# A vision block on one core: first mean, second mean and half of the output projection moved directly behind a block of scores or minima, into another PSUM bank

## The reference

```python
h = h + attention(layernorm(h))     # 16 heads of 16, stablemax3, then w_out, b_out
h = h + ffn(layernorm(h))           # 4 experts of 1024 hidden, relu, weighted by a gate per token
```

## Time and profile before

| | before |
|---|---|
| median of 3 runs | 3930.28 us (3929.3 to 3931.45) |
| profiled execution | 3926.76 us, span 3925.0 us |
| PE busy | 3863.5 us, 98% |
| PE weight loads | 3394.5 us, 86% |
| GpSimd busy | 2819.8 us, 72% |
| VectorE busy | 2817.5 us, 72% |
| ScalarE busy | 2379.7 us, 61% |
| chain that ended last | 95% PE |

### The profile page before, as it was taken

How to read it: one execution, slowest core, us unless ns; L and a number is a source line. 1 busy time by engine, 2 the same in 40 slices (tenths; PEclk the granted TensorE clock), 3 DMA queues, 4 the chain that set the end, 5 groups by cost and what they waited for, 6 DMA issues and landing times.

```text
span 3925.0 us, 86888 instructions
## 1 busy us (share of the span) xinstructions
PE 3863.5 (98%) x30148; PEld 3394.5 (86%) x30148; DVE 2817.5 (72%) x4316; ACT 2379.7 (61%) x4388; POOL 2819.8 (72%) x3543
## 2 busy tenths in 40 slices
PE   7899999999999999999999999999999999999998
PEld 4788888888888888888888888888888888888887
DVE  6777777777777777777777777777777777777763
ACT  5665566655566655666555666556665556665562
POOL 5666777767777667777677776677776777766676
PEclk9999999999999999999999999999999999999999
DMA  7344444444444444444444444444544444444454
GB/s 243 95 136 142 135 134 142 136 140 140 125 140 139 137 139 137 133 144 135 142 138 127 140 139 137 138 134 135 143 135 143 137 129 141 136 140 125 137 149 140
DMA packets 776546, 545.55 MB, mean 139 GB/s; under 512 B 157624, under 2 KB 701752, under 8 KB 775096
## 3 DMA queue, kind: packets, MB, share of 16 engines
q1 hardware_dynamic: 771416, 539.70, 47.0%
q10 hardware_dynamic: 4704, 0.30, 0.1%
HBM read 518.48 MB, written 21.30 MB: 138 GB/s over the span
## 4 chain that ended last, share of the span: by engine, by line
PE 95%; POOL 1%; DVE 1%; ACT 1%; issue 1%; DMA 0%; ACTq 0%; SPq 0%; POOLq 0%; DVEq 0%
PE ps L1343 67%; PE ps L1427 5%; PE ps L1442 5%; PE ps L1456 5%; PE ps L1541 4%; PE ps L1550 3%; PE ps L1558 2%; PE ps L1519 1%; PE ps L1525 1%; PE ps L1531 1%; PE ps L1507 1%; PE ps L1513 1%; ACT probs L716 0%; DVE lows L1052 0%; PE ps L1339 0%
## 5 line engine op out<-in xcount | busy, mean ns | idle before, releaser
L1343 PE MATMUL ps<-xn,w1s 128*128 128x197 f32 x4096 | 909.7, 343 | 4.6 <-ACT hT L681 2.3
L1343 PEld LDWEIGHTS ps<-xn,w1s 128*128 128x128 f32 x4096 | 676.3, 189 | 144.0 <-issue 132.4
L1343 PE MATMUL ps<-hT,w_s 128*128 128x197 f32 x4064 | 783.8, 330 | 7.6 <-issue 7.3
L977 DVE SCALAR_TENSOR_TENSOR probs<-probs,ps 99x788 f32<-99x788 f32 x512 | 483.3, 970 | 322.5 <-ACT probs L716 322.5
L1343 PEld LDWEIGHTS ps<-hT,w_s 128*128 128x128 f32 x4064 | 691.7, 190 | 9.6 <-issue 7.9
L572 POOL TENSOR_TENSOR hT<-hT 128x197 f32<-128x197 f32 x508 | 331.8, 653 | 505.7 <-ACT hT L696 502.5
L1343 PE MATMUL ps<-xt,w1s 128*128 128x197 f32 x3072 | 681.2, 330 | 3.3 <-ACT hT L687 1.7
L565 POOL TENSOR_SCALAR hT<-hT 128x394 f32<-128x394 f32 x512 | 641.2, 1252 | 17.7 <-DVE hT L1099 17.7
L1052 DVE TENSOR_REDUCE lows<-ps 99x8 f32<-99x1576 f32 (+1 forms) x256 | 460.3, 1799 | 218.6 <-PE ps L1442 218.5
L1343 PE MATMUL ps<-hT,w_a 128*128 128x197 f32 x3048 | 591.0, 329 | 0.2 <-DVE yw L1117 0.2
L1343 PEld LDWEIGHTS ps<-xt,w1s 128*128 128x128 f32 x3072 | 538.2, 190 | 35.9 <-DVE hT L1105 3.4
(11 more groups left out here) (142 smaller groups left out, 6196.7 us busy)
## 6 DMA issues: line engine op xcount, KB each, us to landing
w_s<-w_sums SPq DMA_DIRECT2D x508, 256.0 KB, 3.6
w_a<-in_w SPq DMA_DIRECT2D x384, 256.0 KB, 3.3
w1s<-w_sums SPq DMA_DIRECT2D x512, 192.0 KB, 2.6
w1s<-in_w SPq DMA_DIRECT2D x512, 128.0 KB, 2.3
x<-in_xT SPq DMA_DIRECT2D x30, 1188.0 KB, 7.4
w1s<-in_w SPq DMA_DIRECT2D x512, 64.0 KB, 1.9
w1s<-w_sums SPq DMA_DIRECT2D x512, 64.0 KB, 2.0
out_rows<-rows SPq DMA_DIRECT2D x252, 48.0 KB
```

Of the source, the lines that this page charges most:

```text
L977: nc.vector.scalar_tensor_tensor(out=part, in0=part, scalar=3.75, in1=ps[0:HB, 2 * half:2 * half + 2, 0:N], op0=ALU.add, op1=ALU.mult).the ...
L1343: return mm(place, weights, rows, start=start, stop=True, skip_group_check=True)
```

## The change

Only PE's program and the table of banks change; the queues of the other engines stay as they are.
- The first mean stands directly behind the scores of block 1, one slot of experts ahead of its old place, and writes Y1 for pairs from 2 on. It waits for `h_ready` (the embedding's results have left Y1) instead of `read(3)`. The scores of block 2 no longer wait for `hc_ready`.
- The first half of the output projection stands directly behind the minima of block 3, one slot ahead, in Y1 for pairs from 1 on, and waits for `whole_ready` (the weighed values have left Y1). The second half stays where it was, in bank 1.
- The second mean stands directly behind the minima of block 4, one slot ahead, in Y1 for pairs from 1 on, and waits for `h2_ready`.
- `embed_product(pair + 2, 0)` stays where it is and waits for `hc2_ready` (the second mean has left Y1) instead of `whole_ready`. The minima of block 5 no longer wait for `hc2_ready`.

```diff
--- before.py
+++ after.py
@@ -116,9 +116,9 @@
         HOMES = (dict(embed0=U0, embed1=U1, mean=Y0, var=Y1, q00=U0, k00=Y0, q10=U1, k10=Y1, q01=U0, k01=Y0, q11=U1, k11=Y1, v0=U0, v1=U1,
                       low_t0=0, low_t1=U0, out0=U1, out1=U0, mean2=U1, var2=U1, z=Y0),
                  dict(embed0=2, embed1=3, mean=0, var=1, q00=U1, k00=Y0, q10=U1, k10=Y0, q01=U1, k01=Y0, q11=U0, k11=Y0, v0=Y0, v1=Y1,
-                      low_t0=U0, low_t1=U1, out0=0, out1=1, mean2=0, var2=0, z=0),
-                 dict(embed=Y1, mean=0, var=1, q00=0, k00=1, q10=0, k10=1, q01=0, k01=1, q11=0, k11=1, v0=0, v1=0,
-                      low_t0=1, low_t1=1, out0=0, out1=1, mean2=0, var2=0, z=0))
+                      low_t0=U0, low_t1=U1, out0=Y1, out1=1, mean2=Y1, var2=0, z=0),
+                 dict(embed=Y1, mean=Y1, var=1, q00=0, k00=1, q10=0, k10=1, q01=0, k01=1, q11=0, k11=1, v0=0, v1=0,
+                      low_t0=1, low_t1=1, out0=Y1, out1=1, mean2=Y1, var2=0, z=0))
 
         LOW_HOMES = ((U0, 0, U0, 0, U0, U0, U0, U0), (0,) * 8, (0,) * 8)
 
@@ -1679,13 +1679,13 @@
 
                 if has_b:
                     gap(b, 1, read(2))
-                experts(1)
-                if has_f:
-                    mean(f, read(3))
+                if has_f:
+                    mean(f, (h_ready, at(f, 2, 2)))
+                experts(1)
                 experts(1)
 
                 if has_b:
-                    gap(b, 2, read(4), *([(hc_ready, at(f, 1, 1))] if has_f else []))
+                    gap(b, 2, read(4))
                 experts(1)
                 if has_f:
                     variance(f, read(5))
@@ -1753,25 +1753,26 @@
 
                 if has_f:
                     lowest(f, 3, (low_ready, at(f, 8, 3)), (k_ready, at(f, 4, 4)))
-                experts(1)
                 if has_b:
-                    project_out(b, 0, (low_ready, at(f, 8, 4)) if has_f else read(16))
+                    project_out(b, 0, (whole_ready, at(b, 8, 8)))
+                experts(1)
+                if has_b:
                     project_out(b, 1, (low_ready, at(f, 8, 4)) if has_f else read(16))
                 experts(1)
 
                 if has_f:
                     lowest(f, 4, (low_ready, at(f, 8, 4)), (h2_ready, at(b, 2, 2)))
-                experts(1)
                 if has_b:
-                    mean2(b, (low_ready, at(f, 8, 5)) if has_f else (h2_ready, at(b, 2, 2)))
+                    mean2(b, (h2_ready, at(b, 2, 2)))
+                experts(1)
                 if has_f:
                     lows_to_columns(f, 0, (low_ready, at(f, 8, 5)))
                 if pair + 2 < PAIRS:
-                    embed_product(pair + 2, 0, (whole_ready, at(b, 8, 8)))
-                experts(1)
-
-                if has_f:
-                    lowest(f, 5, (low_ready, at(f, 8, 5)), (q_max_ready, at(f, 4, 2)), (hc2_ready, at(b, 1, 1)))
+                    embed_product(pair + 2, 0, (hc2_ready, at(b, 1, 1)))
+                experts(1)
+
+                if has_f:
+                    lowest(f, 5, (low_ready, at(f, 8, 5)), (q_max_ready, at(f, 4, 2)))
                 experts(1)
                 if has_b:
                     variance2(b, (low_ready, at(f, 8, 6)) if has_f else (hc2_ready, at(b, 1, 1)))
```

More of the change, by code:

```diff
@@ L1763, in step @@
                     lowest(f, 4, (low_ready, at(f, 8, 4)), (h2_ready, at(b, 2, 2)))
+                if has_b:
+                    mean2(b, (h2_ready, at(b, 2, 2)))
                 experts(1)
-                if has_b:
-                    mean2(b, (low_ready, at(f, 8, 5)) if has_f else (h2_ready, at(b, 2, 2)))
                 if has_f:
```

## The result

| | before | after |
|---|---|---|
| median | 3929.3 us (5 runs, 3926.92 to 3931.45) | 4012.13 us (5 runs, 4010.94 to 4014.32) |
| profiled execution, span | 3925.0 us | 4012.5 us |
| mean granted clock of TensorE | 0.996 | 0.990 |
| one pair (start of mean2 to the next) | 120.01 us | 122.24 us, in 12 pairs 123.9 |

The ratio is 1.0212, with a 95% interval of 1.0201 to 1.0223. The time lies inside the range on record, 16 us above the forecast of 3996. Two things make up the 83 us, and both can be read in the trace.

What follows compares the result with a forecast made beforehand. PE, without gaps in the middle, was taken to bound the kernel; the embedding's new wait, 29 x 2.28 = 66 us, on 3926.76 gives 3993, or 3996 against the median, which is 3.5 higher; range 3970 to 4030.

Steps and rivals of the forecast that it cites:

- The decisive step: Embedding's wait for centring L1009: mean2 delays VectorE's down sum, product 2.28 us later per pair, 29 times, 66 us.
- What the moves save: Output projection 0.04 and mean2 0.05 us no longer lost: 0.09 per pair, under 3 us in 31 pairs.
- The early places: Inputs ready at the moved pieces' new places, costing nothing; room 1.8 us at first mean, 0.96 at mean2.
- rival (b): PE's clock falls too, 3.4 us per fall: 4095 if every time, 4030 in a third of the pairs; chance 0.10.
- a granted clock under 1.00 in the middle: Sign of being wrong: PE's granted clock below full in the middle of the trace after; no size given.
- its last sign: If PE's busy time, not its idle time, grew, the reading of the switch cost would be wrong.
- the switch cost: Leaving a tiled block on PE costs 0.11 us, paid by the first whole matmul behind it; no saving taken.
- The rows that I leaned on: Rows 7: PE stall of 2.17 us followed by full clock, 2.93 by half clock; forecast's 2.3 judged nearer the first.
- (a): Embedding's wait there, but VectorE's queue not late by mean2: 1.66 us x 29 = 48 us, 3968 to 3978; chance 0.06.
- (c): Embedding doesn't wait at Y1, as the centring ends ahead of it: about 3922 us; chance 0.02.
- (d): Nothing changes: moved products wait as before, embedding's wait masked by another: 3930 us; chance 0.02.

Runs made afterwards that it cites:

- e2: Kernel before, nothing moved, only the new wait added: the first embedding product of pair + 2 also waits for the second mean's centring; 3975.9 us, ratio 1.0121.
- e7: Changed kernel with the second mean's centring on VectorE put behind the down sum and ahead of the weighting; 3977.7 us, ratio 1.0123.
- e3: Changed kernel with the second mean's centring on VectorE put directly behind the minimum of block 4, ahead of both sums and the weighting; 3930.3 us, ratio 1.0002.
- e1: Changed kernel with only the second mean put back to its old place and bank 0, the embedding's new wait gone; 3926.9 us, ratio 0.9997.
- e6: e1 with the first embedding product of pair + 2 issued ahead of the second mean and the transpose; 3927.3 us, ratio 0.9995 to before.
- e5: Changed kernel with the second mean's centring on VectorE one place later, behind the two writes of q_max; 4107.3 us, ratio 1.0452.
- e8: Changed kernel with the second mean's centring on VectorE put between the two writes of q_max; 4017.3 us, ratio 1.0228.
- e10: Changed kernel with the matmul of the first mean done twice, same result; 4017.0 us, ratio 1.0222 to before.

## Why the prediction was right, and what it missed

- **The decisive step held**, "VectorE's work isn't left where it is". Counted from mean2's start, L1117 was forecast at 1892.07 - 1889.08 = 2.99 us and came at 2.97, L1009's end at 5.10 and came at 5.09, the product at 5.32 and came at 5.23, since the release took 0.14 and not 0.22; 2.28 us late a pair forecast, 2.23 measured, 29 times. e2 and e7 show the two parts, e3 that the queue's order is the cause.
- **What the moves save** was put at 0.09 a pair with the 0.11 of leaving a block going over to whatever follows. The trace of the changed kernel shows the 0.11 going over, at all three places. e1 has 0.05 a pair and e6 0.10.
- **The early places** were free as worked out: 0.96 us of room at mean2 forecast and found.
- **The step that fell short is the split between the forecast and rival (b).** I treated them as alternatives, all 29 pairs at full clock or a fall too. In truth the forecast's stall brought a share of (b) with it: 12 pairs, near the "third of the pairs" that set the top of the range. Its price was 1.68 us, not the 3.4 taken from the start of the kernel, where half clock lasted 6.8 us; in e5 and in three of e8's falls it lasts as long again, and 3 us are lost. 66 forecast became 64.7 plus 20.2. The prediction had named a granted clock under 1.00 in the middle as a sign of being wrong, and it came: 0.99 from 240 to 3600 us. PE's busy time, its last sign, grew too, from 3863.5 to 3888.9 us beside some 62 us of idle time; but 20 of these 25 are the passes at half clock, so the switch cost isn't at fault.
- **Some of it is luck.** The direction and the waits, 64.7 us of the loss, were reasoned. That the total lies only 16 us above the forecast is owed to the number of falls, which nothing in the prediction could give: with the same stall e10 has 1 instead of 12. The rows that I leaned on, full clock behind 2.17 and half clock behind 2.93, were read as if the length decided; e8 and e10 show that at these lengths it doesn't.
- **Rivals (a), (c) and (d) are out**: L1117 was released by PE, the centring ended some 2 us after PE had come to its wait, and the wait wasn't masked.

## What to carry to other kernels

When a piece is moved into another bank to lose one wait, ask who reads it there and where that reader stands in its own queue: the next writer of the bank waits for everything that the reading engine does first. Here one call moved on VectorE (e3) takes back 82 of the 83 us, and the gain that was to be had was 0.1 us a pair all along. And where the engine that sets the end gets a stall of two or three microseconds in every period, as here, count the stall in full and leave room for the clock besides: here from nothing to 3 us a pair.

## What the hardware showed that I had not expected

- A stall of 2.13 us in each of 29 pairs was followed by half clock in 12 of them where a pair was 122.24 us long, and in 1, the first, where it was 122.90. At 2.66 us it was 7 (pairs of 122.79, in the slowest of four executions) and 10 (123.44), at 3.20 us 28, at 1.46 and below none.
- Half clock lasted 3.4 us in the changed kernel (1.7 lost) and 6.8 us in e5, 6 of them behind the stall (3 lost).
- One matmul more in each pair, 21 us of work in all, made the changed kernel only 5 us longer (e10).
- Which whole matmul follows a tiled block (one of the 32-row blocks of scores or minima) doesn't matter: 0.11 us each time, for 197 columns (1.11 against 1.00 for six passes) as for 394 (0.77 against 0.66 for mean2).
